# Second layer norms stored unnormalised, and normalised where the rows are loaded

## The chip, the cores and the metric

One core of one Trainium2 chip. The time is device microseconds of one execution. The engines are TensorE (PE; PEld is its weight load), VectorE (DVE), ScalarE (ACT), GpSimd (POOL) and SyncE (SP), which issues most of the transfers.

## The reference

Four graph layers over 100000 nodes of 128 features and 50000 edges, each followed by a layer norm of x plus the layer. The two in the middle have a norm inside as well, so rows pass through two norms in a row:

```
h = norm(agg_bn + x) * ln_gamma + ln_beta      # L1, inner norm
x2 = norm(x1 + relu(h) + x1)                    # L1, outer ("second") norm
y = x_gat @ lin_W + lin_b
h = norm(x2 + y) * ln_g + ln_b                 # L2, inner norm
x3 = norm(x2 + h)                               # L2, outer ("second") norm
x4 = norm(x3 + layer3(x3))                      # layer3: six graph convolutions and a dense layer
```

x2 enters layer L2 as a factor of products (three heads W, the attention scores) and as a residual; x3 enters layer 3 through the product with W1 and as the last residual.

## The kernel before

The graph is sorted by target. Nodes with edges lie in 99 blocks of 512 rows (class "a", four rows of 128 floats for each partition), all nodes once more in 98 blocks of 1024 rows (class "b"). The kernel is a row of passes with a barrier after each. Within a pass each engine has its own list of stages; `pipeline` runs them in ticks: in tick t a stage with lag k handles block t - k, and the stages of a tick run in the listed order. Semaphores tie the engines together, and every engine, SP too, takes its work in order.

The passes that matter here, with their stretch in the profiled execution: the first pass (0 to 660 us, indices, weights, rescaled input); the gated node pass (2945 to 4070: the two norms of layer L1, scores); the attention gather pass (4070 to 4925: layer L2 for class b, and gathers of scores); the softmax pass (to 5007); the attention pass (5007 to 6112: layer L2 for class a); and the passes of layer 3, g3 to g8, of which g5, g6 and g7 (7185 to 8746) carry the last layer of class b beside their own work and g8 (8747 on) that of class a.

In the gated node pass ACT does for each block `normalise_1` (12 activations `Identity(scale*x+bias)`, one for each row of a partition), `normalise_2` (12 more, into o_s), the two square roots and the copies of the turned rows out of PSUM (L1934). POOL does `batch_norm` and `gain`, DVE the statistics, factors, shift, rectify and the scores' copies; TensorE turns the normalised rows and multiplies them by score_w. The rows of o_s are stored as x2.

In the attention gather pass (class b, 8 rows a partition) TensorE turns x2 as loaded (`turn`, lag 1), ACT copies it out (`evacuate`, L2281, lag 2), TensorE multiplies by self_w, DVE adds gat_row (L2250), and statistics, normalise_1, gain, add_x, statistics, normalise_2 follow; the result is stored as x3, turned, multiplied by W1 and stored. POOL adds beta to x2 (`add_beta`, L2152) and gathers the scores.

In the attention pass (class a) ACT weighs the gathered rows by three heads (L2634, `Copy` with a scale), DVE sums runs (L2556) and adds the own part (L2578, gb_u). SP's tick is load, store_sums (768 KB, waits for L2578 of the tick), load_again (x_r of the block before), store, store_next. DVE's `rows` adds gat_row to the product (L2587) and then x_r (L2590), one lag behind load_again.

In layer 3 the residual x3 is loaded into res_s and added in `last_rows` (L1096).

## Time and profile before

| | us |
|---|---|
| median of 3 runs | 9802.32 (9798.62 to 9814.49) |
| the profiled execution | 9807.44 |
| its span | 9805.7 |
| PE busy | 6177.6 (63%) |
| DVE busy | 7307.2 (75%) |
| ACT busy | 5719.7 (58%) |
| POOL busy | 7491.2 (76%) |

Durations come from the profiled execution. Its time beside its span differs by 1.7 us, which lies around the program. The shares are means over passes with different limits. In the rows below, "busy (xN)" is the busy time of an engine and its number of instructions; "[0.5 <-X]" is idle time ahead of a row and what ended it. Rows of a timeline join neighbouring instructions of one kind: the first number is the start of the first, the second reaches to the end of the last. Neighbours on ACT overlap a little, so starts tell how long an instruction holds the engine.

### The profile page before, as it was taken

The page shows a single profiled execution, that of the slowest core. Times are in us where ns is not written, and L with a number is a line of the kernel's source. Part 1 is how long each engine was busy: PE and PEld are TensorE (multiplying, and loading weights), DVE is VectorE, ACT ScalarE, POOL GpSimd, SP SyncE. Part 2 cuts the span into 40 slices and gives each one's busy share as a digit, 9 for nine tenths or more (in the row PEclk, how much of TensorE's full clock was granted, in tenths as well). Part 3 has the DMA queues.
Part 4 walks back from the last instruction along what each step waited for, and adds up shares of the span by engine and source line. Part 5 has one row for each costly group of instructions (what it writes and reads, how often), then busy time and mean ns, then how long its engine had stood idle before and what let it go on. Part 6 is the DMA issues. An engine that isn't in the chain of part 4 may idle for free. (4 is left out here: it accounts for less than half of the span.)

```text
span 9805.7 us, 131503 instructions
## 1 busy us (share of the span) xinstructions
PE 6177.6 (63%) x32436; PEld 5071.6 (52%) x32436; DVE 7307.2 (75%) x22701; ACT 5719.7 (58%) x14065; POOL 7491.2 (76%) x6901
## 2 busy tenths in 40 slices
PE   7017766668875666777736766884467676654444
PEld 3016655557764666677736665782245453432222
DVE  8349989978887777799978887665568776864444
ACT  0016667778878999899948887331135443432222
POOL 7756678878869888688847776776777777777777
PEclk9569988889995555689868888665568656765555
DMA  3999988863337777444435554663346443432222
GB/s 101 333 300 314 317 282 309 307 217 105 107 90 237 242 241 241 157 158 158 153 98 183 185 180 160 172 176 92 95 136 191 131 119 107 147 104 67 67 67 61
DMA packets 1024294, 1693.84 MB, mean 173 GB/s; under 512 B 301775, under 2 KB 544661, under 8 KB 1023474
## 3 DMA queue, kind: packets, MB, share of 16 engines
q1 hardware_dynamic: 797008, 1380.40, 41.2%
q0 software_dynamic: 166560, 199.56, 9.5%
q10 hardware_dynamic: 59970, 105.49, 3.1%
q8 instruction: 270, 4.42, 0.2%
q14 instruction: 486, 3.98, 0.1%
HBM read 988.10 MB, written 707.84 MB: 173 GB/s over the span
## 5 line engine op out<-in xcount | busy, mean ns | idle before, releaser
L1357 POOL DMA_INDIRECT g_got<-scaled,row_src x2352 | 2227.1, 947 | 788.5 <-issue 664.3
L909 DVE SCALAR_TENSOR_TENSOR g_sums<-g_got,first,g_sums 128x128 f32<-128x128 f32 (+3 forms) x3136 | 871.9, 278 | 1142.2 <-DMA g_got<-scaled,row_src 1132.0
L301 PE MATMUL g_a_p_z<-sb_L_gnn_W,g_a_u_t 128*128 128x128 f32 (+3 forms) x2574 | 577.7, 360 | 562.9 <-ACT g_a_u_t L1190 181.9
L913 DVE SCALAR_TENSOR_TENSOR g_sums<-g_sums,cont,g_got 128x128 f32<-128x128 f32 (+3 forms) x3128 | 880.1, 281 | 0.0
L1190 ACT COPY g_a_u_t<-g_a_p_t 128x512 f32<-128x512 f32 (+3 forms) x495 | 225.1, 455 | 1094.4 <-PE g_a_p_t L1142 644.0
L301 PE MATMUL g_bb_p_z<-sb_L_gnn_W,g_bb_u_t 128*128 128x128 f32 (+2 forms) x4302 | 756.4, 336 | 117.6 <-DVE g_bb_z L1075 58.3
L301 PEld LDWEIGHTS g_a_p_z<-sb_L_gnn_W,g_a_u_t 128*128 128x128 f32 (+1 forms) x2574 | 422.6, 235 | 730.9 <-ACT g_a_u_t L1190 402.6
L301 PEld LDWEIGHTS g_bb_p_z<-sb_L_gnn_W,g_bb_u_t 128*128 128x128 f32 x4302 | 666.1, 234 | 175.2 <-issue 146.2
L1190 ACT COPY g_bb_u_t<-g_bb_p_t 128x1024 f32<-128x1024 f32 (+2 forms) x294 | 233.9, 796 | 846.9 <-PE g_bb_p_t L292 843.8
L1514 POOL DMA_INDIRECT cg_got_src<-x,row_src x392 | 502.8, 1283 | 119.5 <-issue 119.5
L2495 POOL DMA_INDIRECT gb_got<-x,row_src x392 | 412.6, 1053 | 228.3 <-POOLq L179 124.3
L461 POOL DMA_INDIRECT f_got<-in_x,idx_dst x396 | 461.8, 1166 | 134.5 <-issue 120.4
L2222 POOL DMA_INDIRECT att_e<-att,row_src x392 | 449.5, 1147 | 141.4 <-issue 98.7
L292 PE MATMUL g_bb_p_t<-ident,g_bb_own 128*128 128x128 f32 x2151 | 358.1, 307 | 308.7 <-DMA g_bb_own<-in_x 216.3
L1357 POOL DMA_INDIRECT g_got<-xs,idx_src x392 | 370.2, 944 | 230.3 <-DVE g_a_own L1028 72.5
L2618 PE MATMUL gb_p_m<-head_w,gb_u_t 128*128 128x128 f32 x2376 | 406.0, 348 | 129.3 <-DVE gb_a_r L2590 121.7
L1257 POOL DMA_INDIRECT out<-g_a_o,idx_out x396 | 390.4, 986 | 120.7 <-issue 120.7
L1357 POOL DMA_INDIRECT g_got<-wide,row_src x392 | 371.8, 949 | 137.3 <-issue 104.2
L1218 ACT ACTIVATE g_bb_o<-g_bb_z 128x1024 f32<-128x1024 f32 (+3 forms) x294 | 196.2, 667 | 471.7 <-DVE g_bb_z L1084 471.6
L292 PEld LDWEIGHTS g_bb_p_t<-ident,g_bb_own 128*128 128x128 f32 x2151 | 286.1, 163 | 356.6 <-DMA g_bb_own<-in_x 229.4
L2618 PEld LDWEIGHTS gb_p_m<-head_w,gb_u_t 128*128 128x128 f32 x2376 | 388.0, 259 | 141.4 <-issue 75.9
L1142 PE MATMUL g_a_p_t<-ident,g_a_own 128*64 128x128 f32 x396 | 104.6, 419 | 465.3 <-DVE g_a_own L1039 465.3
(492 smaller groups left out, 22854.2 us busy)
## 6 DMA issues: line engine op xcount, KB each, us to landing
raw<-gb_u SPq DMA_DIRECT2D x98, 768.0 KB, 3.9
xs<-f_o ACTq DMA_DIRECT2D x97, 516.0 KB
f_x<-in_x ACTq DMA_DIRECT2D x97, 512.0 KB
g_bb_own<-in_x SPq DMA_DIRECT2D x97, 512.0 KB
wide<-g_bb_o SPq DMA_DIRECT2D x97, 512.0 KB
g_bb_own<-wide SPq DMA_DIRECT2D x97, 512.0 KB
g_bb_res<-in_x SPq DMA_DIRECT2D x97, 512.0 KB
x<-g_bb_o SPq DMA_DIRECT2D x97, 512.0 KB
```

The source lines that it names most:

```text
L292: last = nc.tensor.transpose(dst_psum[0:n * k, q * P:q * P + p], tile[0:p, q * g * k:(q * g + n) * k], ident[0:p, 0:p])
L301: last = nc.tensor.matmul(dst_psum[0:p, q * g * width:(q * g + n) * width], turned_tile[0:n * k, q * P:q * P + p], weight[0:n * k, 0:n * w ...
L461: pool.indirect_dma_start(got[b.s4][:, c * D:(c + 1) * D], None, a["x"], bass.IndirectOffsetOnAxis(ap=idx_dst[:, b.n * CH + c:b.n * CH + c ...
L909: nc.vector.scalar_tensor_tensor(out=self.firsts, in0=new, scalar=first[:, col], in1=self.firsts, op0=ALU.mult, op1=ALU.add).then_inc(run_ ...
L913: nc.vector.scalar_tensor_tensor(out=self.part(b.s, c), in0=before, scalar=cont[:, col], in1=new, op0=ALU.mult, op1=ALU.add).then_inc(run_ ...
L1190: last = nc.scalar.copy(to, source)
L1257: nc.gpsimd.indirect_dma_start(self.to, bass.IndirectOffsetOnAxis(ap=idx_out[:, b.n * CH + c:b.n * CH + c + 1], axis=0), self.o_s[b.s4][:, ...
L1357: pool.indirect_dma_start(got[b.s4][:, c * row:(c + 1) * row], None, table, bass.IndirectOffsetOnAxis(ap=index[:, b.n * CH + c:b.n * CH + ...
L1514: pool.indirect_dma_start(got[b.s4][:, c * D:(c + 1) * D], None, x1, bass.IndirectOffsetOnAxis(ap=index[:, b.n * CH + c:b.n * CH + c + 1], ...
L2222: pool.indirect_dma_start(att_e[:, 4 * (b.n * CH + c):4 * (b.n * CH + c + 1)], None, att, bass.IndirectOffsetOnAxis(ap=row_src[:, b.n * CH ...
L2495: pool.indirect_dma_start(got[b.s4][:, c * D:(c + 1) * D], None, x2, bass.IndirectOffsetOnAxis(ap=row_src[:, b.n * CH + c:b.n * CH + c + 1 ...
L2618: last = nc.tensor.matmul(p_m[:, c * D:(c + 1) * D], u_t[h][:, c * P:(c + 1) * P], head_w[:, h * D:(h + 1) * D], start=(h == 0), stop=(h = ...
```

## The change

The second norms are no longer applied before rows are stored. x2 and x3 are stored as the sum before the norm. The factors 1/sd and -mean/sd of every row are kept in four tensors in SBUF (root2, shift2, root3, shift3). Since products with rows that are scaled and shifted alike can be taken with weights whose input means are taken out, head_w, score_w and W1 are centred in the first pass (multiplied by I - 1/128), and the result of a product is scaled by root where it is used: in the scores, in weight_e and weight_own, and in out_rows. The fourth column of the scores' rows carries root2 to the gathers. head_w, self_w and gat_row are centred over their outputs as well, which makes the mean of the inner norm of L2 zero, so that its normalise_1 needs no bias. Where x2 or x3 serves as a residual, a new stage `settle` on ACT normalises it in place after its load, one Identity for each row of a partition; in the attention gather pass the turned rows too are taken after it. o_s goes; y_s holds four blocks and is what is stored and turned, one lag earlier.

The diff, cut to its core (the names of stages and tensors not shown follow from these):

```diff
+                        if pe is not None:
+                            pe.wait_ge(evicted, len(moves))
+                        for t in (*[head_w[:, h * D:(h + 1) * D] for h in range(3)], score_w[:, :], w["L3_gnn_W1"][:, :]):
+                            emit(lambda o, t=t: nc.tensor.matmul(o, centre_in[:, :], t, start=True, stop=True), tuple(t.shape), t)
...
+                            done(nc.vector.tensor_scalar(centre_in[:, :], ident[:, :], -1.0 / D, None, ALU.add))
...
+                            heads_w = head_w[:, :].rearrange("p (h f) -> p h f", f=D)
+                            nc.vector.tensor_reduce(centre_out[:, 0:3], heads_w, AX, ALU.add)
+                            nc.vector.tensor_reduce(centre_out[:, 3:4], self_w[:, :], AX, ALU.add)
+                            done(nc.vector.tensor_reduce(centre_out[:, 4:5], gat_row[:, :], AX, ALU.add))
+                            yield
+                            done(nc.vector.tensor_scalar(centre_out[:, :], centre_out[:, :], 1.0 / D, None, ALU.mult))
+                            yield
+                            nc.vector.tensor_tensor(heads_w, heads_w, per_row(centre_out, P, 3, D), ALU.subtract)
+                            nc.vector.tensor_tensor(self_w[:, :], self_w[:, :], centre_out[:, 3:4].to_broadcast([P, D]), ALU.subtract)
+                            done(nc.vector.tensor_tensor(gat_row[:, :], gat_row[:, :], centre_out[:, 4:5].to_broadcast([P, D]),
+                                                         ALU.subtract))
...
-                nc.vector.wait_ge(m.loaded_c[b.s], (b.pair + 1) * DMA)
+                nc.vector.wait_ge(m.settled, b.n + 1)
...
+            def settle(self, b):
+
+                p, j = self.r.pj(b)
+                m, res = self.m_, self.res_s[b.s]
+                nc.scalar.wait_ge(m.loaded_c[b.s], (b.pair + 1) * DMA)
+                roots, shifts = factor(root3, self.r, b), factor(shift3, self.r, b)
+                for q in range(j):
+                    last = nc.scalar.activation(res[0:p, q * D:(q + 1) * D], res[0:p, q * D:(q + 1) * D], ACT.Identity,
+                                                bias=shifts[:, q:q + 1], scale=roots[:, q:q + 1])
+                last.then_inc(m.settled, 1)
+
...
+                    return self.on(lag, every, (self.normalise, 8), (self.evacuate_b, 2), (self.root, 6), (self.evacuate, 1), (self.settle, 4)), []
...
+                            stages = ahead + in_a((na.normalise, 3), (na.evacuate_b, 1), (na.evacuate, 0), (na.root, 2), (na.settle, 1)) + behind
...
+        root2, shift2, root3, shift3 = (keep(n, [P, NBA * BOTH]) for n in ("root2", "shift2", "root3", "shift3"))
+
+        def factor(t, r, b):
+
+            at = (r.start + b.n) * BOTH + (0 if r.name == "a" else CH)
+            p, j = r.pj(b)
+            return t[0:p, at:at + j]
+
...
-                    sp.wait_ge(m.normed_b, b.n + 1)
-                    sp.dma_start(self.r.rows(x2, b, self.base()), split(self.o_s[b.s], p, j)).then_inc(m.stored[b.s], DMA)
+                    sp.wait_ge(m.summed_b, b.n + 1)
+                    sp.dma_start(self.r.rows(x2, b, self.base()), split(self.y_s[b.n % 4], p, j)).then_inc(own_stored[b.s4], DMA)
...
+                    sp.wait_ge(m.settled, b.n + 1)
...
+                    dve.wait_ge(self.n2.factored, b.n + 1)
+                    roots = factor(root2, self.r, b)
                     if self.a:
-                        nc.vector.tensor_copy(own_src[:, :, bass.ds(b.n * CH, CH)], both.rearrange("p j f -> p f j")[:, 0:3, :])
-                        nc.vector.tensor_copy(own_dst[:, :, bass.ds(b.n * CH, CH)], both.rearrange("p j f -> p f j")[:, 3:6, :])
-                    nc.vector.tensor_copy(split(self.att_s[b.s], p, j, 4)[:, :, 0:3], both[:, :, 0:3]).then_inc(m.attended, 1)
+                        by_head = roots.unsqueeze(1).to_broadcast([p, 3, j])
+                        for to, f in ((own_src, 0), (own_dst, 3)):
+                            nc.vector.tensor_tensor(to[:, :, bass.ds(b.n * CH, CH)], both.rearrange("p j f -> p f j")[:, f:f + 3, :],
+                                                    by_head, ALU.mult)
+                    nc.vector.tensor_tensor(split(self.att_s[b.s], p, j, 4)[:, :, 0:3], both[:, :, 0:3],
+                                            roots.unsqueeze(2).to_broadcast([p, j, 3]), ALU.mult).then_inc(m.attended, 1)
...
-                        act.wait_ge(m.normed_b, b.n - 3)
+                        act.wait_ge(own_stored[b.s4], b.turn * 2 * DMA)
+                        act.wait_ge(m.turned, b.n - 3)
...
-                def normalise_2(self, b):
+                def put_roots(self, b):
                     p, j = self.r.pj(b)
                     m, act = self.m, nc.scalar
                     act.wait_ge(self.n2.factored, b.n + 1)
                     if b.after(2):
-                        act.wait_ge(m.stored[b.s], b.pair * DMA)
-                        act.wait_ge(m.turned, b.n - 1)
-                    self.n2.scale(self.o_s[b.s], self.y_s[b.n % 4], b, self.first, p, j).then_inc(m.normed_b, 1)
+                        act.wait_ge(m.stored_b[b.s], b.pair * DMA)
+                    nc.scalar.copy(split(self.att_s[b.s], p, j, 4)[:, :, 3], factor(root2, self.r, b)).then_inc(m.settled, 1)
 
                 def evacuate(self, b):
...
+                    turn_rows(self.p_x, self.y_s[b.n % 4], p, j, D).then_inc(m.turned, 1)
...
-                                      (na.store, 7, NBA), (nb.store, 7, NB), (na.store_scores, 9, NBA),
+                                      (na.store, 6, NBA), (nb.store, 6, NB), (na.store_scores, 9, NBA),
...
-                        pipeline(dve, [(na.scores, 9, NBA), (nb.scores, 9, NB), (stats_1, 2, NBA), (factors_2, 6, NBA),
+                        pipeline(dve, [(na.scores, 8, NBA), (nb.scores, 8, NB), (stats_1, 2, NBA), (factors_2, 6, NBA),
...
-                                       (na.normalise_2, 6, NBA), (nb.normalise_2, 6, NB), (na.evacuate, 7, NBA),
-                                       (nb.evacuate, 7, NB)])
+                                       (na.evacuate, 6, NBA), (nb.evacuate, 6, NB), (na.put_roots, 7, NBA), (nb.put_roots, 7, NB)])
...
-                        pipeline(pe, [(na.turn, 7, NBA), (nb.turn, 7, NB), (na.score, 8, NBA), (nb.score, 8, NB)])
+                        pipeline(pe, [(na.score, 7, NBA), (nb.score, 7, NB), (na.turn, 6, NBA), (nb.turn, 6, NB)])
...
-                self.n1.factors(self.link_f, b, m.factored)
+                nc.vector.reciprocal(self.n1.rstd[b.s][0:p, 0:j], self.n1.sd[b.s][0:p, 0:j]).then_inc(m.factored, 1)
...
+                nc.vector.reciprocal(roots, self.n2.sd[b.s][0:p, 0:j]).then_inc(m.factor_step_b, 1)
+                nc.vector.wait_ge(m.factor_step_b, self.link_g.count())
+                if self.a:
+                    nc.vector.tensor_tensor(self.by_root[b.s4][:, :], roots, at_window(inv, b), ALU.mult)
+                nc.vector.scalar_tensor_tensor(out=factor(shift3, self.r, b), in0=self.n2.stats[b.s][0:p, 1:3 * j:3], scalar=-1.0,
+                                               in1=roots, op0=ALU.mult, op1=ALU.mult).then_inc(m.factored_b, 1)
...
+                by = self.by_root[b.s4][0:p, 0:j] if self.a else factor(root3, self.r, b)
+                nc.vector.tensor_tensor(g, split(self.p_g, p, j, H1), by.unsqueeze(2).to_broadcast([p, j, H1]), ALU.mult
+                                        ).then_inc(m.finished, 1)
...
+                pool.wait_ge(m.settled, b.n + 1)
...
-            def normalise_2(self, b):
+                if b.after(4):
+                    act.wait_ge(own_stored[b.s4], b.turn * DMA)
+                    act.wait_ge(m.turned_b, b.n - 3)
+                p, j = self.r.pj(b)
+                for q in range(j):
+                    last = nc.scalar.activation(self.y_s[b.s4][0:p, q * D:(q + 1) * D], self.r_s[b.s][0:p, q * D:(q + 1) * D],
+                                                ACT.Copy, scale=self.n1.rstd[b.s][0:p, q:q + 1])
+                last.then_inc(m.normed, 1)
+
+            def settle(self, b):
+
+                p, j = self.r.pj(b)
                 m, act = self.m, nc.scalar
-                act.wait_ge(m.factored_b, b.n + 1)
-                if b.after(2):
-                    act.wait_ge(m.stored[b.s], b.pair * DMA)
-                    act.wait_ge(m.turned_b, b.n - 1)
-                self.n2.scale(self.o_s[b.s], self.y_s[b.n % 3], b).then_inc(m.normed_b, 1)
+                if self.a:
+                    act.wait_ge(m.loaded_b[b.s], (b.pair + 1) * DMA)
+                else:
...
-                pe.wait_ge(m.normed_b, b.n + 1)
+                pe.wait_ge(m.summed_b, b.n + 1)
...
-                            pe.wait_ge(m.loaded[b.n % 3], (b.n // 3 + 1) * DMA)
+                            pe.wait_ge(m.settled, b.n + 1)
...
-                                       (n.evacuate_out, 7, NB), (n.normalise_2, 6, NB)])
+                                       (n.evacuate_out, 7, NB), (n.settle, 1, NB)])
...
+                        by_source = att_e[:, :].rearrange("p (t f) -> p f t", f=4)[:, 3:4, :].to_broadcast([P, H, T])
+                        nc.vector.tensor_tensor(weight_e[:, :, :], weight_e[:, :, :], by_source, ALU.mult)
+                        by_own = root2[:, :].rearrange("p (n g) -> p n g", g=BOTH)[:, :, 0:CH]
+                        for h in range(H):
+                            own_h = split(weight_own[:, h, :], P, NBA, CH)
+                            last = nc.vector.tensor_tensor(own_h, own_h, by_own, ALU.mult)
+                        done(last)
...
+                        pipeline(sp, [(load, 0, NBA), (store_sums, 1, NBE), (load_again, 2, NBA), (n.store, 6, NBA),
...
-                            dve.wait_ge(m.loaded_b[b.s], (b.pair + 1) * DMA)
+                            dve.wait_ge(m.settled, b.n + 1)
...
-                                       (n.normalise_1, 4, NBA), (n.normalise_2, 6, NBA)])
+                                       (n.normalise_1, 4, NBA), (n.settle, 2, NBA)])
```

## Rows read from the trace of the kernel before

**Rows 1.** Stages: busy us of PE, PEld, DVE, ACT, POOL; clock, DMA share, GB/s
```profile
2945.00:4070.00 1125.00, 713.32 (x3534) 687.25 (x3534) 865.32 (x2572) 1084.34 (x2751) 950.02 (x592) 0.53 0.70 232
4070.00:4925.00 855.00, 647.81 (x4692) 626.61 (x4692) 790.02 (x1578) 820.16 (x1957) 706.42 (x490) 0.85 0.45 152
5007.00:6112.00 1105.00, 742.70 (x4742) 686.92 (x4742) 941.54 (x1778) 891.55 (x2562) 835.72 (x789) 0.83 0.54 176
7240.00:8740.00 1500.00, 1018.72 (x3832) 684.53 (x3831) 1165.55 (x4879) 639.62 (x1448) 1148.92 (x1278) 0.69 0.48 140
8740.00:9805.00 1065.00, 508.47 (x1395) 279.28 (x1395) 485.52 (x1596) 307.12 (x694) 819.88 (x887) 0.50 0.24 66
```

**Rows 2.** Timeline of ACT, gated node pass: start, us, line, operation
```profile
3507.27 0.57 ACT L1770 ACTIVATE cn_n_sd<-cn_n_stats,eps 128x12 f32<-128x12 f32 x1
3507.47 1.91 ACT L1784 ACTIVATE cn_a_o<-cn_a_y,cn_n_nmr,cn_n_rstd 128x128 f32<-128x128 f32 x4
...
3512.08 0.84 ACT L1934 COPY cn_a_x_t<-cn_a_p_x 128x512 f32<-128x512 f32 x1
...
3518.49 1.92 ACT L1784 ACTIVATE cn_a_o<-cn_a_y,cn_n_nmr,cn_n_rstd 128x128 f32<-128x128 f32 x4
```

**Rows 3.** Waits, 3050 to 3950 us: total us, times, longest
```profile
DVE cn_consts L1776 <- ACT cn_n_sd L1770: 155.2, 82, 2.5
POOL cn_b_y L1877 <- ACT cn_b_y L1784: 96.8, 81, 1.2
```

**Rows 4.** Timeline of ACT, attention gather pass
```profile
4400.03 3.35 ACT L354 ACTIVATE ga_b_y<-ga_b_r,ga_b_n_nmr,ga_b_n_rstd 128x128 f32<-128x128 f32 x8
4403.11 0.47 ACT L333 ACTIVATE ga_b_n_sd<-ga_b_n_stats,eps 128x8 f32<-128x8 f32 x1
...
4408.39 3.35 ACT L354 ACTIVATE ga_b_y<-ga_b_r,ga_b_n_nmr,ga_b_n_rstd 128x128 f32<-128x128 f32 x8
```

**Rows 5.** Tile gb_a_x_r: who waited (us, times); landing
```profile
  DVE gb_a_r L2590: 80.8, 92
...
DMA to landing us min/median/max: 3.1/4.1/6.0
```

**Rows 6.** Timeline of DVE, attention pass
```profile
5499.92 0.69 DVE L2590 TENSOR_TENSOR gb_a_r<-gb_a_r,gb_a_x_r 128x512 f32<-128x512 f32 x1 [0.50 <-DMA gb_a_x_r<-x]
...
5504.17 1.76 DVE L2578 TENSOR_TENSOR gb_u<-gb_run,gb_own_w 128x1536 f32<-128x1536 f32 x1 [0.24 <-DVE gb_run L2556]
...
5510.56 0.69 DVE L2590 TENSOR_TENSOR gb_a_r<-gb_a_r,gb_a_x_r 128x512 f32<-128x512 f32 x1 [0.64 <-DMA gb_a_x_r<-x]
```

**Rows 7.** Timeline of SP's queue, attention pass
```profile
5506.37 0.38 SPq L2533 DMA_DIRECT2D gb_a_x_r<-x  x1
```

**Rows 8.** Waits, 240 to 660 us
```profile
DVE f_o L771 <- DMA f_inv<-inv_d: 228.1, 77, 11.0
```

**Rows 9.** Timeline of ACT, attention pass
```profile
5500.11 3.61 ACT L2634 ACTIVATE gb_acc<-gb_got,weight_e 128x128 f32<-128x128 f32 x12
5503.62 0.29 ACT L333 ACTIVATE gb_a_n_sd<-gb_a_n_stats,eps 128x4 f32<-128x4 f32 x1
```

**Rows 10.** Timeline of TensorE, attention gather pass
```profile
4402.25 1.04 PE L292 MATMUL ga_p_x<-ident,ga_b_x 128*128 128x128 f32 x8
...
4407.91 1.87 PE L292 MATMUL ga_b_p_o<-ident,ga_b_o 128*128 128x128 f32 x8
```

**Rows 11.** Attention gather pass by line (busy us, mean ns)
```profile
L2152 POOL TENSOR_TENSOR ga_b_x_beta<-ga_b_x,row_L_gnn_ln_b 128x1024 f32<-128x1024 f32 x84 | 221.7, 2639 | 1.3
...
L348 DVE SCALAR_TENSOR_TENSOR ga_b_n_nmr<-ga_b_n_stats,ga_b_n_rstd 128x8 f32<-128x8 f32 x167 | 67.7, 405 | 5.8
```

**Rows 12.** Gated node pass by line (busy us, mean ns)
```profile
L1877 POOL TENSOR_TENSOR cn_b_y<-cn_b_y,cn_half 128x1024 f32<-128x1024 f32 x92 | 216.2, 2350 | 101.6 <-ACT cn_b_y L1784 101.6
```

**Rows 13.** A tile's instructions, softmax pass: ns min/median/max
```profile
L2449 DVE TENSOR_TENSOR weight_own<-sm_run,sm_power_own x1: 1375/1375/1375, 4993.5 to 4993.5; 128x1176 f32<-128x1176 f32 x1
```

**Rows 14.** Waits, 7240 to 8740 us
```profile
POOL g_got L1357 <- issue: 323.3, 1123, 0.3
```

More of the change, by code:

```diff
@@ L1292, in scalar_stages @@
                 if self.deep:
-                    return self.on(lag, every, (self.normalise, 8), (self.evacuate_b, 2), (self.root, 6), (self.evacuate, 1)), []
+                    return self.on(lag, every, (self.normalise, 8), (self.evacuate_b, 2), (self.root, 6), (self.evacuate, 1), (self.settle, 4)), []
                 if self.plain:
@@ L1432, in _ @@
                         if deep:
-                            stages = ahead + in_a((na.normalise, 3), (na.evacuate_b, 1), (na.evacuate, 0), (na.root, 2)) + behind
+                            stages = ahead + in_a((na.normalise, 3), (na.evacuate_b, 1), (na.evacuate, 0), (na.root, 2), (na.settle, 1)) + behind
                         elif normal:
@@ L1803, in __init__ @@
                     self.y_s = [sb(f"{n}_y{s}", [P, G * D]) for s in range(4)]
-                    self.o_s = [sb(f"{n}_o{s}", [P, G * D]) for s in two]
                     self.att_s = [sb(f"{n}_att{s}", [P, G * 4]) for s in two]
@@ L1983, in _ @@
                         nb.stores_done()
+                        for s in range(UNROLL):
+                            sp.wait_ge(own_stored[s], (blocks_in(NBA, s, UNROLL) + blocks_in(NB, s, UNROLL)) * DMA)
                     @block.gpsimd
@@ L2056, in __init__ @@
                 self.r_s = [sb(f"{n}_r{s}", [P, G * D]) for s in two]
-                self.y_s = [sb(f"{n}_y{s}", [P, G * D]) for s in range(3)]
-                self.o_s = [sb(f"{n}_o{s}", [P, G * D]) for s in two]
+                self.y_s = [sb(f"{n}_y{s}", [P, G * D]) for s in range(4)]
+                self.by_root = [sb(f"{n}_by_root{s}", [P, G]) for s in range(UNROLL)]
                 self.g_s = [sb(f"{n}_g{s}", [P, G * H1]) for s in two]
@@ L2085, in stores_done @@
                 for s in range(2):
-                    nc.sync.wait_ge(self.m.stored[s], blocks_in(self.r.blocks, s) * DMA)
                     nc.sync.wait_ge(self.m.stored_b[s], blocks_in(self.r.blocks, s) * DMA)
+                for s in range(UNROLL):
+                    nc.sync.wait_ge(own_stored[s], blocks_in(self.r.blocks, s, UNROLL) * DMA)
             def stats_1(self, b):
@@ L2165, in normalise_1 @@
                 act.wait_ge(m.factored, b.n + 1)
-                if b.after(3):
-                    act.wait_ge(m.normed_b, b.n - 2)
-                self.n1.scale(self.y_s[b.n % 3], self.r_s[b.s], b).then_inc(m.normed, 1)
-            def normalise_2(self, b):
-                m, act = self.m, nc.scalar
-                act.wait_ge(m.factored_b, b.n + 1)
-                if b.after(2):
-                    act.wait_ge(m.stored[b.s], b.pair * DMA)
-                    act.wait_ge(m.turned_b, b.n - 1)
-                self.n2.scale(self.o_s[b.s], self.y_s[b.n % 3], b).then_inc(m.normed_b, 1)
+                if b.after(4):
+                    act.wait_ge(own_stored[b.s4], b.turn * DMA)
+                    act.wait_ge(m.turned_b, b.n - 3)
+                p, j = self.r.pj(b)
+                for q in range(j):
[3 more added lines that the diff above has]
+            def settle(self, b):
+                p, j = self.r.pj(b)
+                m, act = self.m, nc.scalar
+                if self.a:
+                    act.wait_ge(m.loaded_b[b.s], (b.pair + 1) * DMA)
+                else:
+                    act.wait_ge(m.loaded[b.n % 3], (b.n // 3 + 1) * DMA)
+                x = self.x_r[b.s if self.a else b.n % 3]
+                roots, shifts = factor(root2, self.r, b), factor(shift2, self.r, b)
+                for q in range(j):
+                    last = nc.scalar.activation(x[0:p, q * D:(q + 1) * D], x[0:p, q * D:(q + 1) * D], ACT.Identity,
+                                                bias=shifts[:, q:q + 1], scale=roots[:, q:q + 1])
+                last.then_inc(m.settled, 1)
             def evacuate_out(self, b):
@@ L2188, in turn_out @@
                 m, pe = self.m, nc.tensor
[L2189 removed]
+                pe.wait_ge(m.summed_b, b.n + 1)
                 if b.after(1):
@@ L2502, in gather_firsts @@
                             if at_end(b):
-                                for s in range(UNROLL):
-                                    pool.wait_ge(raw_stored[s], blocks_in(NBE, s, UNROLL) * DMA)
+                                for s in two:
+                                    pool.wait_ge(sums_stored[s], blocks_in(NBE, s) * DMA)
                                 pool.indirect_dma_start(firsts[:, :], None, raw,
```

75 lines of the change are left out of this document (33 added, 42 removed).

## The prediction

> **What bounds the kernel now.** The kernel is a row of passes with a barrier between them, so I read it by stage. The table of stages [rows 1] gives each pass its busy time per engine; the reader is to see that a different engine is full in each. In the gated node pass ACT is busy 1084.34 of 1125 us and TensorE is granted 0.53. In the attention gather pass ACT is busy 820.16 of 855 and DVE 790.02. In the attention pass no engine is full: DVE, the busiest, has 941.54 of 1105. In the stretch of g5 to g7 DVE and POOL are level, and in g8 POOL is far ahead (819.88 of 1065).
>
> Then the waits and the timelines. In the gated node pass a block takes 11.02 us: na's normalise_2 starts at 3507.47 and again at 3518.49, and ACT's instructions stand back to back [rows 2]. DVE waits there for ACT 155.2 us in 82 blocks, 1.89 us each, and POOL 96.8 us in 81, 1.195 each [rows 3]. So POOL is the next limit, at 11.02 - 1.195 = 9.83 us. In the attention gather pass a block takes 4408.39 - 4400.03 = 8.36 us, again with ACT back to back [rows 4].
>
> The attention pass needs more care. The tile view of the second load of x2 says DVE waited for its landing before L2590 in 92 blocks, 80.8 us, and that the load lands 4.1 us after its issue (3.1 to 6.0) [rows 5]. Read as a loop of one tick: L2590 starts at 5499.92 (the add of x_r), then statistics, run sums, and the sum L2578, which ends at 5504.17 + 1.76 = 5505.93 [rows 6]; only then does SP, which waits for that sum before its raw store and takes its work in order, issue the next x_r load, at 5506.37 [rows 7]; it lands and L2590 starts at 5510.56. The loop is 6.01 + 0.44 + 4.19 = 10.64 us, and it is what sets the pass. Everything else fits beside it.
>
> **The change part by part.** The profiled execution took 9807.44 us (span 9805.7, 1.7 us around it); the median of the runs is 9802.32, 5.1 below. I sum against 9807.4 and take 5 off at the end.
>
> *First pass.* Five more matmuls, five copies and eight small DVE instructions over 128 rows, in steps woven between the rescaling blocks. I count some 59 steps before and 67 after, in 98 blocks, so none spills over the end. DVE waits there 228.1 us for loads [rows 8]. Cost 0; were the cover gone, about 18 instructions under a microsecond each, 10 us.
>
> *Gated node pass.* normalise_2 goes from ACT: 12 activations, from 3507.47 to 3512.08, 4.61 us a block. put_roots adds two small ones; a small activation holds ACT 0.20 us (3507.27 to 3507.47) [rows 2], so 0.4. ACT comes to 11.02 - 4.61 + 0.4 = 6.8 us. The saving is not 4.2 but what POOL had idle, 1.195 us: nothing of gain and batch_norm changes. 98 blocks give -117 us. DVE keeps 1.89 - 1.195 = 0.7 us idle, which covers the scores' multiplies in place of copies, on the same elements. The new wait in normalise_1 (the store and the transposes of the block four before) stands one tick behind them; ACT has 3 us idle now, and the traffic rises from a share of 0.70 [rows 1] to 0.70 x 11.02 / 9.83 = 0.79. The last block's normalise_2 leaves the tail: -5. Bounds: 0 for the saving if the transfers took over, -185 (DVE's 1.89) at the far end, which POOL forbids; I take POOL's.
>
> *Attention gather pass.* Three edits. normalise_1 becomes a Copy with only a scale. An Identity with scale and bias takes (4403.11 - 4400.03) / 8 = 0.385 us [rows 4], the Copy with a scale in the attention pass (5503.62 - 5500.11) / 12 = 0.2925 [rows 9]: 8 x 0.0925 = -0.74 us on ACT. normalise_2's eight Identities are replaced by settle's eight: 0. DVE loses a scalar_tensor_tensor of mean 405 ns [rows 11].
>
> But settle stands last in ACT's tick and the transposes of the same block now wait for it, while evacuate, first in ACT's next tick, waits for all eight transposes. Before, these waited only for a load. ACT must stand still between settle's end and the transposes' end. Eight transposes take 1.04 us at the higher clock and 1.87 in the other case [rows 10]; the stage is granted 0.85, 0.7 of the way from 0.5 to 1, so 0.7 x 1.04 + 0.3 x 1.87 = 1.29. With 0.1 for two hand-overs and 0.1 for the overlap of neighbouring activations that is lost (estimates; 0 to 0.3 together), 1.49. A block comes to 8.36 - 0.74 + 1.49 = 9.11: +0.75, over 98 blocks +73 us. Bounds 8.86 (+49) and 9.7 (+131). DVE, at 790.02 / 98 = 8.06 less 0.3, stays under it.
>
> Here a second-order cost is possible. POOL's add_beta takes 2639 ns in this pass, and the small L348 instruction 405 ns on average [rows 11] though its median is 169; in the gated node pass the same size of POOL addition takes 2350 [rows 12]. So the two engines hold each other up. The Trainium skill (SBUF — State Buffer, "SBUF: two separate sides") says that a VectorE instruction with two SBUF inputs and a GpSimd instruction that reads SBUF exclude each other for a whole instruction; gain and add_x are such. By this rule the gated node pass, whose VectorE inputs of that kind come from PSUM, keeps its saving, and the gather pass can lose more (a rival below).
>
> *Softmax pass.* One multiply over 128x1176, like L2449's 1.375 us [rows 13], and three over a third of it, 0.5 each: +3, on the path, as DVE works alone there. Bounds 2 to 6, for the strided operand.
>
> *Attention pass.* ACT's work falls by 4 x 0.0925 and normalise_2's four activations become settle's four. What counts is the place. settle(b) waits for the x_r load, is last in ACT's tick, and L2590 of the next tick now waits for settle. It goes into the loop between the landing and L2590: 4 x 0.385 + 0.1 = 1.64, and a hand-over of 0.06: 10.64 + 1.7 = 12.3 us. ACT is free when the load lands (its other work, evacuations, 12 weighings, a root, normalise_1, ends some 7 us after the previous settle), so the cost is the full 1.7 and not more; the add_beta on POOL also waits for settle, but is used a tick or more later. 97 blocks give +165 us. Bounds: a landing at the shortest 3.1 takes 1.0 off, +68; 1.9 a block, +185, at the other end.
>
> *Layers 3.* settle puts 8 activations (3.1 us) a block into three passes and 4 (1.6) into the last. ACT is busy there 639.62 of 1500 and 307.12 of 1065 us [rows 1], and POOL's gathers set the pace: in the 1500 us its busy 1148.92 and the 323.3 between gathers that are issued back to back [rows 14] come to 1472. Four gather buffers lie between it and the rest. Cost 0, with +1 for the tail; uncovered, 98 x 3.1 = 304.
>
> Sum: -117 - 5 + 73 + 3 + 165 + 1 = +120; 9807.4 + 120 = 9927, and less 5 for the median, **9922 us**.
>
> **The rivals.** (A) The attention pass absorbs settle. For it: DVE's wait at L2590 is only 0.88 us, and a longer tick leaves the transfer more room, so that x_r may land 1.7 us sooner after its issue. It decides once the landing takes under 2.5 us. Against: the load is issued behind the 768 KB raw store, and the shortest landing of all is 3.1. It gives 9922 - 165 = 9757, faster. (B) TensorE falls to its lower clock in the gather pass, as it is in the gated node pass at a similar busy share. Then its work, 647.81 / 98 = 6.6 us at 0.85, is 11.2 at 0.5 and over ACT's 9.11: +205, 10127. Against: its busy share hardly changes. (C) DVE's two-input instructions and add_beta, which now waits for settle, meet in every block: 8.06 + 2.35 = 10.4 us, +127, 10049. Against: ACT's tick of 9.1 leaves DVE room to fall beside it. It is the Trainium skill's rule on that port pair (SBUF — State Buffer, the section named above) at its worst. (D) The gather pass does not stall at all and follows DVE at 7.9: -45 in place of +73, 9804, no change. Against: the order of the stages shows no other work for ACT in that gap.
>
> **How the numbers follow.** Forecast 0.67, A 0.12, B 0.08, C 0.08, D 0.05. The difference that can be told is about 0.2% (20 us). Slower is forecast, B and C: 0.83; same is D: 0.05; faster is A: 0.12. The range leaves out A and B (0.2) and holds D and C: 9800 to 10060.
>
> **What would show it.** Gated node: 9.8 us a block, ACT idle about 3, POOL without waits. Gather pass: ACT idle before the copy of ga_x_t, ended by PE, about 1.3 to 1.6 a block. Attention pass: L2590 waits for ACT, tick 12.3, while the x_r landing stays near 4. Layers 3: same length to a few us. If the attention pass stays under 1130 us, the loop is read wrong; if the gated node pass stays over 1050, transfers bound it.

## The result and the profile after

The changed kernel takes 10051.01 us (median of 4, 10041.63 to 10055.52) against 9802.68 for the kernel before: a ratio of 1.025, 95% interval 1.0232 to 1.0268. It is slower, as forecast, and within the range, but by 248 us and not by 120. The profiled spans differ by 10039.9 - 9805.7 = 234.2 us, and the passes, each from its first instruction to that of the next, share this out:

```
pass              before    after   difference   forecast
up to gated node  2945.6   2943.4      -2           0
gated node        1124.9    999.7    -125        -117 - 5
gather             852.1    993.5    +141         +73
softmax             84.5     88.2      +4          +3
attention         1113.8   1292.5    +179        +165
g3, g4            1066.5   1065.4      -1           -
g5                 519.0    539.2     +20           0
g6                 520.5    537.6     +17           0
g7, g8            1578.6   1580.3      +2          +1
```

The table of stages after, the one that answers to [rows 1] (the last two stretches are g5 and g6); columns are busy us of PE, PEld, DVE, ACT and POOL, then clock, DMA share and GB/s:

```profile
2943.00:3942.00 999.00, 743.42 (x3534) 706.67 (x3534) 863.79 (x2572) 680.15 (x1770) 945.94 (x592) 0.54 0.81 261
3942.00:4935.00 993.00, 729.23 (x4692) 706.83 (x4692) 727.25 (x1468) 761.38 (x1956) 629.64 (x490) 0.78 0.45 131
5022.00:6315.00 1293.00, 804.93 (x4754) 769.55 (x4754) 900.58 (x1783) 852.82 (x2563) 831.71 (x789) 0.76 0.45 151
7379.00:7920.00 541.00, 374.05 (x1486) 258.81 (x1486) 417.60 (x1738) 352.53 (x804) 396.70 (x441) 0.75 0.57 168
7920.00:8457.00 537.00, 385.08 (x1223) 250.91 (x1223) 367.47 (x1647) 298.72 (x726) 396.62 (x441) 0.54 0.38 106
```

In the gated node pass ACT fell from 1084 us to 680 and POOL is now full, with 946 of 999. In the gather pass and the attention pass no engine is full: ACT has 761 of 993, DVE 901 of 1293. That is how a chain of waits looks in such a table. The busy times of ACT, DVE and POOL fell in both passes; what these engines gained is idle time. TensorE alone is busy longer: 729 us in place of 648 in the gather pass, for the same 4692 matmuls, at a granted clock of 0.78 in place of 0.85, and 805 in place of 743 in the attention pass, at 0.76 in place of 0.83.

POOL's timeline in the gated node pass of the kernel after: one instruction, once a block, starts 9.83 us apart, and its instructions between stand back to back.

```profile
3504.35 2.38 POOL L1918 TENSOR_TENSOR cn_b_y<-cn_b_y,cn_half 128x1024 f32<-128x1024 f32 x1
3506.66 1.30 POOL L1904 TENSOR_TENSOR cn_a_v<-cn_a_sum,bn_scale 128x512 f32<-128x512 f32 x1
...
3512.95 1.26 POOL L1918 TENSOR_TENSOR cn_a_y<-cn_a_y,cn_half 128x512 f32<-128x512 f32 x1
3514.18 2.34 POOL L1918 TENSOR_TENSOR cn_b_y<-cn_b_y,cn_half 128x1024 f32<-128x1024 f32 x1
```

ACT's timeline in the gather pass after, two blocks, beside [rows 4]. The bracket is idle time and what ended it.

```profile
4401.12 1.01 ACT L2339 COPY ga_x_t<-ga_p_x 128x1024 f32<-128x1024 f32 x1 [1.19 <-PE ga_p_x L292]
...
4402.23 2.44 ACT L2217 ACTIVATE ga_b_y<-ga_b_r,ga_b_n_rstd 128x128 f32<-128x128 f32 x8
...
4405.66 3.19 ACT L2232 ACTIVATE ga_b_x<-ga_b_x,shift,root 128x128 f32<-128x128 f32 x8
4410.23 1.01 ACT L2339 COPY ga_x_t<-ga_p_x 128x1024 f32<-128x1024 f32 x1 [1.38 <-PE ga_p_x L292]
...
4415.24 1.01 ACT L2242 COPY ga_b_o_t<-ga_b_p_o 128x1024 f32<-128x1024 f32 x1 [1.27 <-PE ga_b_p_o L292]
4416.15 3.19 ACT L2232 ACTIVATE ga_b_x<-ga_b_x,shift,root 128x128 f32<-128x128 f32 x8
```

The reader is to see two gaps. The one before L2339 is in every block: settle (L2232) ends, TensorE turns the block, ACT copies it. The one before L2242 is in some blocks only. The starts of settle give the length of a block: 8.92 us in 20 of the 40 blocks that I read in four stretches, 9.5 to 11.2 in the other 20, 9.73 on average. TensorE in the same two blocks, beside [rows 10]:

```profile
4399.99 1.09 PE L292 MATMUL ga_p_x<-ident,ga_b_x 128*128 128x128 f32 x8 [2.24 <-ACT ga_b_x L2232]
4400.92 1.90 PE L301 MATMUL ga_b_p_g<-sb_L_gnn_W,ga_b_o_t 128*128 128x64 f32 x16
4402.65 1.04 PE L292 MATMUL ga_b_p_o<-ident,ga_b_y 128*128 128x128 f32 x8
...
4408.90 1.29 PE L292 MATMUL ga_p_x<-ident,ga_b_x 128*128 128x128 f32 x8 [3.42 <-ACT ga_b_x L2232]
4409.98 3.52 PE L301 MATMUL ga_b_p_g<-sb_L_gnn_W,ga_b_o_t 128*128 128x64 f32 x16
4413.29 1.91 PE L292 MATMUL ga_b_p_o<-ident,ga_b_y 128*128 128x128 f32 x8
```

The same sixteen matmuls take 1.90 us in the short block and 3.52 in the long one, behind a longer wait for ACT. The rows of these two blocks, from one start of settle to the next, tell that the granted clock (the first of the last three columns) was 1.00 in the short one, which is TensorE's higher level of 2.4 GHz, and 0.69 in the long one, which ran in part at the lower level of 1.2 GHz:

```profile
4396.74:4405.66 8.92, 6.50 (x58) 6.12 (x56) 6.09 (x12) 7.74 (x21) 5.08 (x5) 1.00 0.50 149
4405.66:4416.15 10.49, 7.25 (x38) 7.25 (x39) 8.76 (x20) 7.84 (x21) 7.43 (x7) 0.69 0.43 128
```

It is so over the whole pass: the short blocks have a mean granted clock of 0.92 and the long ones of 0.70. ACT's waits over 4020 to 4850 us, 85 blocks:

```profile
ACT ga_x_t L2339 <- PE ga_p_x L292: 124.2, 85, 2.1
...
ACT ga_b_o_t L2242 <- PE ga_b_p_o L292: 47.0, 41, 1.3
```

The attention pass after: DVE's timeline, SP's queue and ACT's settle, beside [rows 6] and [rows 7], and what the view of the tile gb_a_x_r says of its landing.

```profile
5602.04 0.69 DVE L2657 TENSOR_TENSOR gb_a_r<-gb_a_r,gb_a_x_r 128x512 f32<-128x512 f32 x1 [3.05 <-ACT gb_a_x_r L2232]
...
5606.28 1.76 DVE L2645 TENSOR_TENSOR gb_u<-gb_run,gb_own_w 128x1536 f32<-128x1536 f32 x1 [0.24 <-DVE gb_run L2623]
...
5614.38 0.69 DVE L2657 TENSOR_TENSOR gb_a_r<-gb_a_r,gb_a_x_r 128x512 f32<-128x512 f32 x1 [2.88 <-ACT gb_a_x_r L2232]
```

```profile
5608.06 0.32 SPq L2605 DMA_DIRECT2D raw<-gb_u  x1
5608.48 0.38 SPq L2600 DMA_DIRECT2D gb_a_x_r<-x  x1
```

```profile
5612.63 1.65 ACT L2232 ACTIVATE gb_a_x_r<-gb_a_x_r,shift,root 128x128 f32<-128x128 f32 x4 [3.72 <-DMA gb_a_x_r<-x]
```

```profile
DMA to landing us min/median/max: 2.7/4.3/6.3
```

One can walk round the loop: the sum ends at 5608.04, the raw store is issued, then the load at 5608.48; it lands, settle runs from 5612.63 to 5614.28, and DVE goes on at 5614.38. This tick is 12.34 us, 1.70 more than the 10.64 of before.

### The profile page after: what moved, and what is told of

It is laid out like the page before. It is cut to its first block and busy times, and to the rows that moved or that the text cites. A ratio compares the mean times of both kernels' runs of the same rounds, so it can differ in the third digit from the quotient of the medians.

```text
span 10039.9 us, 131555 instructions
## 1 busy us (share of the span) xinstructions
PE 6385.6 (64%) x32446; PEld 5276.4 (53%) x32446; DVE 7207.4 (72%) x22620; ACT 5656.3 (56%) x14262; POOL 7409.4 (74%) x6901
## 5 line engine op out<-in xcount | busy, mean ns | idle before, releaser
L1544 POOL DMA_INDIRECT cg_got_src<-x,row_src x392 | 472.1, 1204 | 119.5 <-issue 119.5
L2582 POOL TENSOR_TENSOR gb_own_w<-gb_a_x,weight_own 128x512 f32<-128x512 f32 x297 | 305.7, 1057 | 305.6 <-DMA gb_a_x<-x 305.5
L2280 POOL DMA_INDIRECT att_e<-att,row_src x392 | 398.6, 1017 | 133.3 <-issue 94.8
L2685 PE MATMUL gb_p_m<-head_w,gb_u_t 128*128 128x128 f32 x2376 | 458.9, 379 | 39.1 <-ACT gb_u_t L2710 21.2
L2685 PEld LDWEIGHTS gb_p_m<-head_w,gb_u_t 128*128 128x128 f32 x2376 | 446.3, 292 | 44.5 <-ACT gb_u_t L2710 33.0
```

The lines of the kernel that those rows point to most:

```text
L1544: pool.indirect_dma_start(got[b.s4][:, c * D:(c + 1) * D], None, x1, bass.IndirectOffsetOnAxis(ap=index[:, b.n * CH + c:b.n * CH + c + 1], ...
L2280: pool.indirect_dma_start(att_e[:, 4 * (b.n * CH + c):4 * (b.n * CH + c + 1)], None, att, bass.IndirectOffsetOnAxis(ap=row_src[:, b.n * CH ...
L2685: last = nc.tensor.matmul(p_m[:, c * D:(c + 1) * D], u_t[h][:, c * P:(c + 1) * P], head_w[:, h * D:(h + 1) * D], start=(h == 0), stop=(h = ...
```

## The experiments

The length of each pass, from its first instruction to that of the next, gives each run's effect, in us:

```
run                      gated  gather  attention    g5      g6     ratio to before [95%]
before                  1124.9   852.1    1113.8   519.0   520.5    1
after                    999.7   993.5    1292.5   539.2   537.6    1.0250 [1.0232, 1.0268]
e1_gb_load_first         998.5  1003.3    1038.7   537.2   540.3    0.9987 [0.9976, 0.9998]
e2_ga_settle_first      1000.6   794.7    1285.3   542.4   537.3    1.0038 [1.0018, 1.0057]
e3_no_last_settle       1001.4   998.7    1289.2   519.8   521.9    1.0219 [1.0189, 1.0249]
e4_before_load_first    1124.4   852.0    1043.9   519.6   521.2    0.9929 [0.9907, 0.9952]
e5_last_settle_earlier  1000.8   999.1    1289.1   519.1   521.3    1.0204 [1.0185, 1.0223]
e7_ga_filled             998.8   959.7    1297.0   536.9   533.9    1.0204 [1.0186, 1.0223]
e8_cn_half_gain          922.9  1001.6    1292.6   541.3   540.6    1.0174 [1.0156, 1.0193]
e6_all_three            1001.1   791.8    1038.9   519.4   521.8    0.9743 [0.9730, 0.9756]
```

Where an edit doesn't touch them, the gather and the attention pass repeat within 12 us and g5 and g6 within 7; that is the grain of this table. The passes are read from one profiled execution of each kernel; the ratios rest on 2 to 8 executions of it, against runs of the kernel before on the same chip (medians 9802.68 for after, 9811.66 for e1 to e4 and 9810.56 for the others).

### The attention pass: the load ahead of the raw store

```diff
-                        pipeline(sp, [(load, 0, NBA), (store_sums, 1, NBE), (load_again, 2, NBA), (n.store, 6, NBA),
+                        pipeline(sp, [(load, 0, NBA), (load_again, 2, NBA), (store_sums, 1, NBE), (n.store, 6, NBA),
```

> The changed kernel, with one edit in the attention pass: SP issues load_again (x_r) ahead of store_sums in its tick, so the load of x_r no longer waits for DVE's sum of the tick. Loop theory: the block of 12.34 us is DVE sum, SP issue, landing behind the raw store, settle, L2657; without it DVE's own 9.5 us set the pass, which falls from 1290 to 960-1000 us; the whole from 10051 to about 9740. Rival, ACT's or TensorE's work in the pass (its clock fell from 0.83 to 0.76) makes the 184 us: the pass stays above 1200 and the whole above 9950.

Measured: 9800.57 us, the attention pass 1038.7, 254 us less, from two stages exchanged in SP's list. The load is now issued 7 us before the raw store, and DVE no longer waits for it. SP's queue and DVE's timeline in this run:

```profile
5600.43 0.39 SPq L2600 DMA_DIRECT2D gb_a_x_r<-x  x1
5607.36 0.32 SPq L2605 DMA_DIRECT2D raw<-gb_u  x1
```

```profile
5601.34 0.69 DVE L2657 TENSOR_TENSOR gb_a_r<-gb_a_r,gb_a_x_r 128x512 f32<-128x512 f32 x1
...
5607.25 0.41 DVE L2189 TENSOR_TENSOR gb_a_g<-gb_a_p_o,gb_a_by_root 128x256 f32<-128x256 f32 x1
5607.58 0.17 DVE L2172 RECIPROCAL root<-gb_a_n_sd 128x4 f32<-128x4 f32 x1
5607.79 0.61 DVE L2175 TENSOR_TENSOR gb_a_by_root<-root,inv 128x4 f32<-128x4 f32 x1
...
5611.28 0.69 DVE L2657 TENSOR_TENSOR gb_a_r<-gb_a_r,gb_a_x_r 128x512 f32<-128x512 f32 x1
```

This tick is 9.94 us and DVE's instructions stand back to back. So the loop through SP's queue set the pass, and the work of ACT and TensorE, the rival, did not. The size was missed: 960 to 1000 us were expected for the pass and 9740 for the whole, from 9.5 us of DVE's work a block. DVE is busy 950 us here and 901 in the kernel after, and most of that difference is one small instruction, L2175 in these rows, that is held up in each block (see the last section). The same exchange in the kernel before:

> The kernel before, with the same swap in SP's tick of the attention pass. Loop theory: its loop of 10.64 us had only a 0.64 us wait of DVE in it, so the swap gives 60 us (0.6 x 98) and the pass falls from 1106 to about 1040; the whole to about 9740. Rival: DVE's wait there was covered by something else a little later, and less than 20 us come.

Measured: 9743.01 us, the pass 1043.9, 70 us less. So the loop set the pass before the change too. Once the load is out of the loop the two kernels' attention passes are level (1038.7 and 1043.9, within the grain of the table): settle's own work costs nothing that can be seen there. Its price was its place between the landing and DVE's addition.

### The gather pass: settle first in ACT's tick

```diff
-                        pipeline(act, [(evacuate, 2, NB), (n.root_2, 6, NB), (n.normalise_1, 4, NB), (n.root_1, 3, NB),
-                                       (n.evacuate_out, 7, NB), (n.settle, 1, NB)])
+                        pipeline(act, [(n.settle, 1, NB), (evacuate, 2, NB), (n.root_2, 6, NB), (n.normalise_1, 4, NB), (n.root_1, 3, NB),
+                                       (n.evacuate_out, 7, NB)])
```

With this, settle of a block is followed by evacuate of the block before, whose transposes are done. The copy that needs this block's own transposes comes in the next tick.

> The changed kernel, with one edit in the attention gather pass: settle is ACT's first stage of a tick and not its last, so that the transposes that wait for it run beside ACT's other work. Stall theory: ACT's idle before the copy of ga_x_t (1.46 us a block) and what follows from it go, and the pass follows ACT and DVE, 7.6 to 8.1 us a block: 990 falls to 770-820 us, the whole to about 9870. Rival, TensorE at its lower clock sets the pass by its own work (6.6 us at 0.85, up to 11.2): the pass stays above 900.

Measured: 9846.32 us, the pass 794.7. ACT's timeline in this run:

```profile
4404.24 3.20 ACT L2232 ACTIVATE ga_b_x<-ga_b_x,shift,root 128x128 f32<-128x128 f32 x8
4407.33 1.00 ACT L2339 COPY ga_x_t<-ga_p_x 128x1024 f32<-128x1024 f32 x1
4408.22 0.32 ACT L333 ACTIVATE ga_b_n_sd<-ga_b_n_stats,eps 128x8 f32<-128x8 f32 x1
4408.43 2.45 ACT L2217 ACTIVATE ga_b_y<-ga_b_r,ga_b_n_rstd 128x128 f32<-128x128 f32 x8
...
4411.85 3.21 ACT L2232 ACTIVATE ga_b_x<-ga_b_x,shift,root 128x128 f32<-128x128 f32 x8
```

No brackets: a block is 7.61 us, which is the forecast's 8.36 - 0.74 without any stall. The place of settle, and what followed from it, turned a gain of 57 us into a loss of 141. The row of the pass in this run:

```profile
3949.00:4742.00 793.00, 641.05 (x4692) 620.53 (x4692) 722.59 (x1468) 748.09 (x1956) 643.07 (x490) 0.85 0.53 164
```

The granted clock is back at the 0.85 of before, though the edit gives TensorE no work.

### The gather pass: is the clock a part of it?

The forecast for a block was 9.11 us and the pass +73; the pass lost twice that. The filler keeps TensorE at work in its wait for settle, on results that are overwritten:

```diff
+                            if b.after(1):
+                                pe.wait_ge(m.evacuated, b.n)
+                            for q in range(12):
+                                at = q % j * P
+                                nc.tensor.transpose(p_x[0:P, at:at + P], ident[:, :], ident[:, :])
                             pe.wait_ge(m.settled, b.n + 1)
-                            if b.after(1):
-                                pe.wait_ge(m.evacuated, b.n)
```

> The changed kernel, and in the attention gather pass TensorE runs 12 transposes of the identity (results overwritten) in each block while it waits for settle, 1.6 us at the higher clock, in a gap of 2.2 to 3.4 us. Theory of the clock: the pass lost twice what was forecast because TensorE's granted clock fell from 0.85 to 0.78; with the gap filled the clock comes back to 0.9 or more, every block is of the short kind (9.1 us), ACT's second wait (for the transposes of the output, 0.55 us a block) goes, and the pass falls from 993 to 890 to 920 us. Rival, theory of hand-overs: the stall is settle, transposes, copy, in that order, whatever the clock; the pass stays at 980 to 1000. If the filler itself is in the way, the pass is over 1000.

Measured: the pass 959.7, with 1176 more matmuls in it. That is 34 us less than in the kernel after, which has the shortest of the five passes of this form; the others take 999 to 1003. The stage's row in this run (it starts some 6 us before the pass and so counts 12 matmuls of the pass before):

```profile
3942.00:4910.00 968.00, 796.43 (x5880) 769.82 (x5878) 731.16 (x1483) 762.39 (x1961) 614.20 (x490) 0.85 0.45 134
```

The clock came back from 0.78 to the 0.85 that the stage had before, not to the 0.9 expected, and blocks of 8.92 us are now 28 of 43 where they were 20 of 40. Neither theory got its number: the clock is a part of the loss, since extra work on TensorE alone made the pass shorter, but the filler removed only some of the long blocks. In those that stayed the granted clock is again 0.70 on average, against 0.96 in the short ones, so they are long at a lower clock as before; why it still fell in them is not shown. The gap to the 907 us that a pass of short blocks alone would take (852.1 + 98 x 0.56) closed by 34 of 86.

### Layer 3: without settle, and with settle earlier

e3 leaves settle out of layer 3: the last residual stays unnormalised there.

> The changed kernel without settle in layer 3: the last residual is added as loaded, unnormalised, so this part of the output is left out. Theory: settle on ACT is what makes g5 and g6 longer, by 21 and 17 us, from the point on at which the four gather buffers are used up; without it eight ticks take 41.6 us to the end, g5 and g6 are 519 and 520 us, g8 does not change, the whole falls by 38 to about 10013. Rival, something else (the larger range of SBUF, the barrier): g5 and g6 stay at 541 and 537.

Measured: g5 519.8 and g6 521.9, as before the change; g8 1057.1, which had not moved. So settle is the cause of the 37 us. Whether it is its work or its place:

```diff
-                    return self.on(lag, every, (self.normalise, 8), (self.evacuate_b, 2), (self.root, 6), (self.evacuate, 1), (self.settle, 4)), []
+                    return self.on(lag, every, (self.normalise, 8), (self.settle, 4), (self.evacuate_b, 2), (self.root, 6), (self.evacuate, 1)), []
```

> The changed kernel with one edit: in ACT's order of the layer-3 passes g5 to g7, settle (8 activations on the residual of the last norm) stands before the evacuation of the second transposes (evacuate_b) and not last. The run without settle showed that it costs g5 and g6 about 18 us each. Theory of place: the time was lost because settle began right after evacuate_b, which had waited 3.3 us for TensorE, and so ended late for DVE's last addition; put into that wait it costs nothing, and g5 and g6 come back from 539 and 538 to 519 to 524 us, the whole to about 10015. Rival, theory of work: 3.1 us more a block on ACT is what costs, wherever it stands: g5 and g6 stay at 535 to 540, the whole at 10051.

Measured: 10010.32 us, g5 519.1 and g6 521.3. All the work of settle is there and nothing is lost: its place was the cause. The kernel after has this on ACT and DVE in g5:

```profile
7830.93 1.11 ACT L1222 ACTIVATE g_bc_h_t<-g_bc_p_t,col_L_gnn_b 128x1024 f32<-128x1024 f32 x1 [3.33 <-PE g_bc_p_t L1183]
7831.94 3.17 ACT L1232 ACTIVATE g_bc_res<-g_bc_res,shift,root 128x128 f32<-128x128 f32 x8
```

```profile
7835.21 1.23 DVE L1115 TENSOR_TENSOR g_bc_y<-g_bc_p_z,g_bc_res 128x1024 f32<-128x1024 f32 x1 [2.52 <-ACT g_bc_res L1232]
```

and in all of g5 up to 7900 us DVE waited so for settle 12 times, which it does not in e5:

```profile
DVE g_bc_y L1115 <- ACT g_bc_res L1232: 25.9, 12, 2.5
```

ACT stood idle for 3.33 us until TensorE had turned the rows, copied them, and only then settled; DVE's last addition waited 2.52 us for it. Who pays is seen in POOL's waits in g5, first in the kernel after (7379 to 7920 us), then in before (7185 to 7704), then in e5 (7379 to 7900):

```profile
POOL g_got L1387 <- DVE g_sums L1063: 16.3, 10, 3.1
```

```profile
POOL g_got L1357 <- DVE g_sums L1044: 2.3, 8, 0.3
```

```profile
POOL g_got L1387 <- DVE g_sums L1063: 1.6, 7, 0.3
```

POOL, which issues the gathers and sets the pace, waited for DVE to free gather buffers. In g6 it waited 17.5 us in 8 such waits, and before the change in none.

### The gated node pass: is it POOL now?

```diff
+                    y = y[:, :, 0:D // 2]
-                    nc.gpsimd.tensor_tensor(y, y, row_of(half[:, 0:D], p, j), ALU.mult).then_inc(m.gained, 1)
+                    nc.gpsimd.tensor_tensor(y, y, row_of(half[:, 0:D // 2], p, j), ALU.mult).then_inc(m.gained, 1)
```

> The changed kernel, but POOL's multiplication by the gain in the gated node pass covers only half of the columns (the other half is left unmultiplied), some 1.2 us less in a block. Theory: POOL sets this pass now (busy 945.94 of 999 us); it falls until DVE's 863.79 is full, from 1000 to 900 to 925 us. Rival: transfers, or the loop from the scores to their load, bound it at 1000 already; then it stays within 10 us of 1000.

This kernel leaves out the gain on half of the columns. Measured: the pass 922.9 (from 999.7). Its row:

```profile
2943.00:3870.00 927.00, 705.35 (x3543) 667.87 (x3543) 864.69 (x2584) 672.37 (x1771) 790.12 (x592) 0.58 0.88 281
```

POOL set it, as the forecast said: with 156 us less on POOL the pass is 77 us shorter, and DVE's 864.69 of 927 is now the fullest. The transfers are not the bound at a share of 0.81, since they went to 0.88.

### All three orders together

> The changed kernel with three changes of order and none of work: settle first in ACT's tick in the attention gather pass, the second load of x2 ahead of the raw store in SP's order in the attention pass, settle before evacuate_b in g5 to g7. If the three losses are separate, each pass is as in its own run: gated node 1000, gather 795, attention 1039, g5 and g6 520 to 539 each. Against before (1125, 852, 1114, 537, 530 by first starts, 519, 521) that is -125 - 57 - 75 and +0 to +36, so 9550 to 9590 us, ratio 0.973 to 0.978. Against the kernel before with only the SP order changed (9743) it is faster by 150 to 190. Rival: the passes share something (the transfers, the clock) and the savings do not add: over 9620.

Measured, five runs: 9558.50 us (9554.26 to 9560.41), ratio 0.9743, 95% 0.9730 to 0.9756. Every pass is as in its own run within the grain, so the three losses were separate. It is 493 us faster than the change as it was made, from the order of the same instructions, 252 faster than the kernel before and 185 faster than e4, the kernel before with its own exchange. Its stages, gated node, gather and attention:

```profile
2945.00:3944.00 999.00, 741.79 (x3534) 705.33 (x3534) 863.83 (x2568) 680.33 (x1770) 946.44 (x592) 0.54 0.81 261
3946.00:4737.00 791.00, 658.38 (x4692) 638.99 (x4692) 720.23 (x1468) 747.44 (x1956) 640.51 (x490) 0.82 0.54 164
4825.00:5863.00 1038.00, 714.88 (x4754) 657.44 (x4754) 951.53 (x1780) 852.74 (x2563) 869.98 (x789) 0.86 0.56 188
```

ACT is as busy as in the kernel after, and an engine is nearly full in each stage again; DVE in the attention pass has 952 us against 901, as in e1. The gather pass is as short as in e2 (791.8 and 794.7) though its granted clock is 0.82 and not 0.85: with the matmuls off ACT's path the somewhat lower clock cost nothing here.

## Why the prediction was right or wrong

The direction and the mechanism were right: the gated node pass gains what POOL had idle, and the two passes of layer L2 give back more. The sum was +120 and the spans differ by +234. The terms:

- **First pass, 0**: -2, right. **Softmax pass, +3**: +4, right.
- **Gated node pass, -117 - 5**: -125. POOL's period of 9.83 us is the forecast one to the hundredth, POOL waits for nobody, and e8 shows that it is the bound. The transfers' share came to 0.81 against the 0.79 worked out.
- **Attention pass, +165**: +179, the right mechanism and 14 us too small. The loop was read rightly from [rows 5 to 7]: its tick grew by 1.70 us, as forecast, e1 broke it and e4 showed it in the kernel before. The mean block grew by 179 / 98 = 1.82; the landing's median went from 4.1 to 4.3 us. Rival A, that the transfer lands sooner and absorbs settle, fell: it landed no sooner.
- **Gather pass, +73**: +141. This is the term that was mis-sized most, by 68 us. The step "ACT must stand still between settle's end and the transposes' end" is right, and e2 shows that without it the block is 7.61 us. That its size was met (124.2 / 85 = 1.46 us a block against 1.49) is in part luck: the wait is 1.19 us in every short block, which so takes 8.92 us and not the forecast 9.11, and 1.71 on average in the long ones. What failed is that the clock entered only into this one stall, and at the stage's old mean of 0.85. The stall gives TensorE 2.2 to 3.4 us of idle time in each block; the stage was granted 0.78, and half of the blocks ran at 0.70 on average. Then the second transposes came late too, and ACT waited for them, 47.0 us in 41 blocks, a wait that the sum did not have. Short blocks alone are 98 x (8.92 - 8.36) = +55; the other 86 us are the long blocks (the trace has 50 of them, 82 us over 8.92 in sum). Rival B, a fall of the clock priced at +205 and given 0.08, was right in part: the argument against it was that TensorE's busy share hardly changes, and it did hardly change (0.76 before, 0.73 after), but the clock fell all the same. Its mechanism, TensorE's own work as the bound, is not what the rows show: in the long block TensorE stood idle for 3.42 us and waited for ACT. The lower clock did its harm through ACT's waits. e7 supports the clock's part but took away only 34 of the 86 us; why the clock still fell in the blocks that stayed long is open. Rival C, DVE and POOL holding each other up, was not seen (add_beta's median is 2.36 us against 2.64 before, and in e2, where its mean is 2.59 again, the block is still 7.61). D, no stall at all, is what e2 got, but only by moving the stage.
- **Layer 3, cost 0**: +37 in g5 and g6, 0 in g7 and g8. The step that failed is "four gather buffers lie between it and the rest". The share of ACT's busy time was read as room, but settle stood behind an evacuation that waits for TensorE, so a ready residual reached DVE late (e5). g5 and g6 lost about 20 us each, and the buffers were not enough cover. That they took the slip in part and then ran out is argued, not shown, and why g7 lost nothing was not tried.

Of the 114 us that the sum lacked, the gather pass is 68, layer 3 is 37 and the attention pass 14, with the others at -5. So the steps that failed are these: the gather pass was summed without ACT's second wait and with the clock at its old mean, layer 3 was put at nothing because of the gather buffers, and the attention loop was sized from a single tick, which grew by 1.70 us where the mean grew by 1.82.

## What to carry to other kernels

When a stage is added to a pipeline, its work is a small part of the question; ask what stands ahead of it in its engine's order, and how soon behind it in time its consumer is. Here 493 us lay in the order of three lists. In an in-order queue of transfers, let a load that needs nothing stand ahead of a store that waits for compute; otherwise load, landing and everything put behind the landing can form a loop, as here. And where a new stall falls on TensorE, price all its work in that pass at the lower clock as well, not only the stalled piece.

## What the runs showed of the hardware

**A clock that follows the order of another engine's list.** With settle last in ACT's tick the gather stage has a granted clock of 0.78, and the same sixteen matmuls take 1.90 or 3.52 us; with settle first, and the same instructions, it has 0.85 (e2) or 0.82 (e6). In the first order, 12 transposes a block in TensorE's idle time (e7) brought it to 0.85 and made the pass 34 us shorter.

**A small DVE instruction held by a GpSimd one.** In e1 L2175, a product of two 128x4 tiles in SBUF, takes 0.61 us, from 5607.79 to 5608.40; in the kernel after it takes 0.16. POOL's addition in e1 covers just this time:

```profile
5607.10 1.26 POOL L2198 TENSOR_TENSOR gb_a_x_beta<-gb_a_x_r,row_L_gnn_ln_b 128x512 f32<-128x512 f32 x1
```

It ends at 5608.36. The two DVE instructions that began under the same addition with only one input from SBUF, L2189 (the other is from PSUM) and the reciprocal L2172, kept their 0.41 and 0.17 us. So did L2645, the sum whose gb_run lies in PSUM: it ran beside POOL's additions in e1 and took 1.76 us, as in the kernel after. Over all blocks the view of the tile has a median of 619 ns in e1 and of 163 in the kernel after (min/median/max):

```profile
L2175 DVE TENSOR_TENSOR gb_a_by_root<-root,inv x99: 161/619/1248, 5105.2 to 6064.8; 128x4 f32<-128x4 f32 x99
```

```profile
L2175 DVE TENSOR_TENSOR gb_a_by_root<-root,inv x99: 161/163/198, 5105.1 to 6304.9; 128x4 f32<-128x4 f32 x99
```

This is the rule of the Trainium skill (SBUF — State Buffer, "SBUF: two separate sides"): a VectorE instruction with two SBUF inputs and a GpSimd instruction that reads SBUF exclude each other for a whole instruction. The trace agrees; the price here is some 0.45 us a block, an estimate of 44 us in 98 blocks of a pass that DVE fills (619 less 163 ns from the two rows above; no run tried to remove it).
